# Weights read in place at register addresses, instead of through a staging tile that GpSimd fills

## The chip, the cores and the metric

The kernel runs on one core of one Trainium2 chip. The metric is the time of one execution on the device in microseconds (us); lower is better.

## The reference, cut to what matters

Two layers of a graph network run over 6250 nodes and 100000 edges, each followed by a residual sum and a layer norm. The change lies in the first one:

```python
msg_1 = x @ W_m1.T + b_m1                 # 6250 x 96, one row for each node
msg_2 = x @ W_m2.T + b_m2
msg_e = edge_attr @ W_me.T + b_me
msg = relu(msg_1[row] + msg_2[col] + msg_e)        # row is src, col is dst
msg = relu(msg @ W_net.T + b_net)                  # 100000 x 96
agg = segment_max(msg, row, num_segments=6250)
out = x @ W_o1.T + b_o1 + (agg @ W_o2.T + b_o2)
```

## The kernel before, in words

Each stage of the kernel is a block in which the five engines run programs of their own, tied by semaphores. `pipeline` (L46) writes such a program: each engine has stage functions with a lag, step t calls each of them for item t - lag, the first steps and the last ones are written out, and those between are a hardware loop whose body holds four steps. In the written-out steps the values that waits compare with are constants; in the loop an instruction computes most of them (`wait`, L89, its `wait_ge` on L92).

An earlier stage (its loop runs from about 190 to 1170 us) has put the edges in the order of their source node, cut into 832 chunks of 128 edges, each of them within one block of 128 nodes. For each edge it has stored `msg_2[col] + msg_e` in DRAM (`edge_in_src_order`), and each edge's node within its block in `src_row`.

The stage that changes is the src-ordered one (L1363 on, 1205 to 1700 us). It has G = 832 / 4 = 208 steps of four chunks each:

- SyncE loads 512 rows of `edge_in_src_order` (`u_in`, L1397) and the broadcast node numbers (`rowt`, L1395).
- VectorE makes the one-hot `oh` (node against edge, L1423) and `same` (L1425).
- GpSimd reads the four block starts of the step from `sf_row` into registers (`offsets`, L76, its load on L78) and copies the block's slice of `m1` into the staging tile `m1_s` (L1411), one copy for each chunk. `m1` is `msg_1` of all nodes, kept in SBUF as three bf16 limbs of F = 96 columns side by side; the copy moves them as 144 f32 words.
- TensorE (`pre`, L1451) transposes `u_in` into a PSUM bank (`turn_u`, L1447) and adds to it, for each of four chunks, three products of a limb as weights and the one-hot as the moving operand (L1458): 12 products of 128 columns. ScalarE applies the relu (L1483). TensorE multiplies by `W_net` (`net`, L1465), VectorE scans the running maximum (L1434), TensorE transposes it (`turn`, L1471), ScalarE copies it out and stores it (L1489, L1493).

TensorE calls in step t: `net` for t - 3, `turn` for t - 5, `pre` for t - 1. Before L1458 it waits for `oh_ready` (L1454) and `m1_ready` (L1455). Buffers are four deep in SBUF and two deep in PSUM.

TensorE already uses register addresses for moving operands elsewhere: in the edge stage (`product`, L1254: L1262 and L1266) and in the last large stage (`pre`, L1784: L1791 and L1796).

Of the kernel before, what the change touches and what calls it, by code (L numbers as in the profile page):

```python
# [15 lines left out]
P = 128  # L16
# [3 lines left out]
F32 = mybir.dt.float32  # L20
BF16 = mybir.dt.bfloat16
# [54 lines left out]
def offsets(nc, engine, row, last):  # L76

    _, values = nc.values_load_multi_w_load_instructions(row, engines=[engine], min_val=0, max_val=last,  # L78
                                                         skip_runtime_bounds_check_because="the table holds block starts only")
    return values  # L80
# [8 lines left out]
def wait(eng, sem, value):  # L89

    if not (isinstance(value, int) and value <= 0):
        eng.wait_ge(sem, value)  # L92

def pass_waits(eng, passed):

    eng.sem_inc(passed, 1)
# [24 lines left out]
def gnn(nc, E, x, xT, src, dst, edge_attr, wm12, bm12, w_e, w_net, b_net, wo1, wo2, bo,  # L122
# [34 lines left out]
    def sb(scope, name, shape, dt=F32):  # L157
        return scope.enter_context(nc.sbuf_tensor(name, shape, dt))
# [4 lines left out]
    def sem(scope, name):  # L163
        return scope.enter_context(nc.semaphore(name))
# [4 lines left out]
    with whole:  # L169
# [53 lines left out]
        with layer0:  # L223
# [1139 lines left out]
            with ExitStack() as t:  # L1363
# [1 line left out]
                rowt = sb(t, "rowt", [P, 4, LEAD + 4 * P], BF16)  # L1365
                same = sb(t, "same", [F, 4, 4 * P], BF16)
                oh = sb(t, "oh_b", [P, 4, 4 * P], BF16)
                m1_s = sb(t, "m1_s", [P, 4, 4, 3 * F // 2])
                msg = sb(t, "msg", [F + 1, 4, 4 * P])
                top = sb(t, "top", [F, 4, 4 * P])  # L1370
                row = sb(t, "row", [P, 4, 4, F])
# [2 lines left out]
                ps_top = [ps(t, f"ps_top{k}", [P, 4, P]) for k in range(2)]  # L1374
                u_in = [sem(t, f"u_in{k}") for k in range(4)]
                row_in = [sem(t, f"row_in{k}") for k in range(4)]
                m1_ready = sem(t, "m1_ready")
                passed_pool = sem(t, "passed_pool")
                one_set = sem(t, "one_set")
                oh_ready = sem(t, "oh_ready_b")  # L1380
                same_ready = sem(t, "same_ready")
# [8 lines left out]
                with nc.Block() as block:  # L1390
                    @block.sync
                    def _(sp):
                        def load(i, u, n):
                            wait(sp, same_ready, i - 3)
                            sp.dma_start(rowt[:, u, :], bcast(loc_d[0:1, bass.ds(4 * P * i, LEAD + 4 * P)], P, LEAD + 4 * P)).then_inc(row_in[u], 16)  # L1395
                            wait(sp, u_turned, i - 3)
                            sp.dma_start(u_in_s[:, u], u_d[bass.ds(4 * P * i, 4 * P), :].rearrange("(j p) f -> p j f", p=P)).then_inc(u_in[u], 16)  # L1397

                        pipeline(sp, G, [(0, load)])

                    @block.gpsimd
                    def _(pool):
                        nc.gpsimd.memset(msg[F:F + 1].rearrange("f u e -> f (u e)"), 1.0).then_inc(one_set, 1)

                        def stage(i, u, n):

                            wait(pool, pre_ready, i - 3)
                            pass_waits(pool, passed_pool)
                            at = offsets(nc, mybir.EngineType.Pool, sf_row[0:1, bass.ds(4 * i, 4)], (NB - 1) * 3 * F // 2)
                            for j in range(4):  # L1410
                                last = nc.gpsimd.tensor_copy(m1_s[:, u, j, :], m1[:].bitcast(F32)[:, bass.ds(at[j], 3 * F // 2)])  # L1411
                            last.then_inc(m1_ready, 1)
                        pool.wait_ge(one_set, 1)
                        pipeline(pool, G, [(0, stage)])

                    @block.vector
                    def _(dve):
                        v = nc.vector

                        def onehot(i, u, n):  # L1420
                            dve.wait_ge(row_in[u], 16 * (n + 1))
                            wait(dve, pre_ready, i - 3)
                            v.tensor_scalar(oh[:, u, :], rowt[:, u, LEAD:], node_c[:], None, ALU.is_equal).then_inc(oh_ready, 1)  # L1423
                            wait(dve, top_ready, i - 3)
                            v.tensor_tensor(same[:, u, :], rowt[0:F, u, LEAD:], rowt[0:F, u, LEAD - 1:LEAD - 1 + 4 * P],  # L1425
                                            ALU.is_equal).then_inc(same_ready, 1)

                        def scan(i, u, n):
                            dve.wait_ge(net_ready, i + 1)
                            dve.wait_ge(same_ready, i + 1)  # L1430
                            wait(dve, top_turned, i - 3)
                            wait(dve, top_ready, i)
                            first = isinstance(i, int) and i == 0
                            v.tensor_tensor_scan(top[:, u, :], same[:, u, :], ps_net[u % 2][:],  # L1434
                                                 0.0 if first else top[:, (u - 1) % 4, 4 * P - 1:4 * P],
                                                 ALU.mult, ALU.max).then_inc(top_ready, 1)
                        pipeline(dve, G, [(4, scan), (0, onehot)])

                    @block.tensor
                    def _(pe):  # L1440
                        m = nc.tensor

                        def turn_u(i, u, n, to):
                            pe.wait_ge(u_in[u], 16 * (n + 1))
                            wait(pe, msg_ready, i - 1)
                            for j in range(4):
                                mm = m.matmul(to[:, P * j:P * j + P], u_in_s[:, u, j, :], ident[:],  # L1447
                                              start=(j == 0), stop=False, is_transpose=True, skip_group_check=True)
                            mm.then_inc(u_turned, 1)

                        def pre(i, u, n):  # L1451
                            to = ps_pre[u % 2]
                            turn_u(i, u, n, to)
                            pe.wait_ge(oh_ready, i + 1)  # L1454
                            pe.wait_ge(m1_ready, i + 1)  # L1455
                            for j in range(4):
                                for k in range(3):
                                    mm = m.matmul(to[:, P * j:P * j + P], m1_s[:, u, j, :].bitcast(BF16)[:, F * k:F * k + F], oh[:, u, P * j:P * j + P],  # L1458
                                                  start=False, stop=(k == 2), skip_group_check=True)
                            mm.then_inc(pre_ready, 1)  # L1460

                        def net(i, u, n):
                            wait(pe, top_ready, i - 1)
                            pe.wait_ge(msg_ready, i + 1)
                            m.matmul(ps_net[u % 2][:], wnet_s[:], msg[:, u, :], start=True, stop=True).then_inc(net_ready, 1)  # L1465

                        def turn(i, u, n):
                            pe.wait_ge(top_ready, i + 1)
                            wait(pe, row_ready, i - 1)
                            for j in range(4):  # L1470
                                mm = m.transpose(ps_top[u % 2][:, j, 0:F], top[:, u, P * j:P * j + P], ident[0:F, 0:F])  # L1471
                            mm.then_inc(top_turned, 1)
                        pe.wait_ge(one_set, 1)
                        pipeline(pe, G, [(3, net), (5, turn), (1, pre)])

                    @block.scalar
                    def _(act):
                        s = nc.scalar

                        def first(i, u, n):  # L1480
                            act.wait_ge(pre_ready, i + 1)
                            wait(act, net_ready, i - 3)
                            s.activation(msg[0:F, u, :], ps_pre[u % 2][:], ACT.Relu).then_inc(msg_ready, 1)  # L1483

                        def rows(i, u, n):
                            act.wait_ge(top_turned, i + 1)
                            s4, n4 = past(row_out, u, n, 4)
                            wait(act, s4, 16 * n4)
                            s.copy(row[:, u], ps_top[u % 2][:, :, 0:F]).then_inc(row_ready, 1)  # L1489

                        def store(i, u, n):
                            act.wait_ge(row_ready, i + 1)
                            act.dma_start(s_d[bass.ds(4 * P * i, 4 * P), :].rearrange("(j p) f -> p j f", p=P), row[:, u]).then_inc(row_out[u], 16)  # L1493
                        pipeline(act, G, [(6, store), (5, rows), (1, first)])
                        for k in range(4):
                            act.wait_ge(row_out[k], 16 * len(range(k, G, 4)))
# [574 lines left out]
```

## Time and profile before

| | us |
|---|---|
| median of 3 runs | 2836.42 |
| lowest, highest | 2833.95, 2842.11 |
| span of the profiled execution | 2838.6 |
| busy in it: TensorE / its weight loads | 2320.7 / 2014.7 |
| VectorE / ScalarE / GpSimd | 2036.0 / 1000.7 / 1860.7 |

The profiled execution is one of its own; only its span is given, and it lies inside the runs. The rows further down come from it.
### The profile page before, as it was taken

The page shows a single profiled execution, that of the slowest core. Times are in us where ns is not written, and L with a number is a line of the kernel's source. Part 1 is how long each engine was busy: PE and PEld are TensorE (multiplying, and loading weights), DVE is VectorE, ACT ScalarE, POOL GpSimd, SP SyncE. Part 2 cuts the span into 40 slices and gives each one's busy share as a digit, 9 for nine tenths or more (in the row PEclk, how much of TensorE's full clock was granted, in tenths as well). Part 3 has the DMA queues.
Part 4 walks back from the last instruction along what each step waited for, and adds up shares of the span by engine and source line. Part 5 has one row for each costly group of instructions (what it writes and reads, how often), then busy time and mean ns, then how long its engine had stood idle before and what let it go on. Part 6 is the DMA issues. An engine that isn't in the chain of part 4 may idle for free. (4 is left out here: it accounts for less than half of the span.)

```text
span 2838.6 us, 89638 instructions
## 1 busy us (share of the span) xinstructions
PE 2320.7 (82%) x22430; PEld 2014.7 (71%) x22431; DVE 2036.0 (72%) x9631; ACT 1000.7 (35%) x2286; POOL 1860.7 (66%) x2595
## 2 busy tenths in 40 slices
PE   7778888888888888799999988876677777777777
PEld 6578777777777777477777766766677666777777
DVE  8678777777777777777787877566666666666666
ACT  7334333333333333144444447222222222222225
POOL 1047777777777777654444437677777777777774
PEclk9789999999999999899999998899999999999999
DMA  5021111111111111188888973222222222222221
GB/s 187 29 57 47 45 45 45 45 45 45 45 45 45 45 45 48 35 218 228 226 226 225 227 194 78 54 54 54 54 54 54 53 54 54 54 55 54 55 53 46
DMA packets 582003, 236.10 MB, mean 83 GB/s; under 512 B 512256, under 2 KB 553772, under 8 KB 581676
## 3 DMA queue, kind: packets, MB, share of 16 engines
q1 hardware_dynamic: 298020, 98.53, 15.3%
q0 software_dynamic: 52736, 93.92, 11.6%
q10 hardware_dynamic: 231176, 42.79, 7.5%
q8 instruction: 34, 0.56, 0.1%
q14 instruction: 37, 0.30, 0.0%
HBM read 142.39 MB, written 98.65 MB: 85 GB/s over the span
## 5 line engine op out<-in xcount | busy, mean ns | idle before, releaser
L1041 POOL DMA_INDIRECT edge_in_src_order<-u,place x784 | 756.6, 965 | 259.9 <-issue 185.2
L1714 POOL DMA_INDIRECT a_rows<-src_table,idx x782 | 742.2, 949 | 248.8 <-issue 237.9
L1791 PE MATMUL ps_h<-a_rows,ident 128*128 x1664 | 237.8, 286 | 247.3 <-SPq L1723 185.4
L1791 PEld LDWEIGHTS ps_h<-a_rows,ident 128*128 128x128 f32 x1664 | 202.6, 192 | 278.9 <-issue 278.7
L1411 POOL COPY m_s<-m 128x144 f32 x832 | 234.0, 325 | 244.0 <-PE ps_pre L1458 242.9
L1831 ACT ACTIVATE h<-ps_h 128x512 f32<-128x512 f32 x208 | 124.2, 597 | 743.6 <-PE ps_h L1796 653.9
L1760 DVE TENSOR_SCALAR ohd_f<-iota_b,dloc_c 128x128 f32<-128x128 bf16 x832 | 199.1, 312 | 209.8 <-PE ps_s L1805 204.1
L1434 DVE TENSOR_TENSOR_SCAN top<-same,top,ps_net 96x512 f32<-96x512 bf16 x207 | 264.1, 1276 | 97.9 <-PE ps_net L1465 97.6
L1335 ACT COPY u<-ps_u 128x384 f32<-128x384 f32 x196 | 93.7, 478 | 604.1 <-DMA edge_in_src_order<-u,place 581.7
L1258 PE MATMUL ps_u<-we_s,attrT 128*128 128x384 f32 x392 | 173.8, 525 | 158.9 <-ACT u L1335 158.9
L1748 DVE TENSOR_TENSOR hsumT<-hsumT,ps_s 128x128 f32 x832 | 238.2, 286 | 84.4 <-DVE deg L1750 1.8
L1796 PE MATMUL ps_h<-bpart,dstT_b 128*128 x1664 | 240.5, 289 | 1.6 <-ACT dstT_b L1825 1.6
L1262 PEld LDWEIGHTS ps_u<-m,dstT 128*128 128x128 f32 x1568 | 193.2, 192 | 66.8 <-issue 63.0
L1805 PE MATMUL ps_s<-ohd_f,h 128*128 128x128 f32 x1664 | 224.5, 279 | 0.5 <-DVE deg L1750 0.3
L1465 PE MATMUL ps_net<-msg,wnet_s 97*96 97x512 f32 x416 | 218.5, 607 | 0.0
L1266 PE MATMUL ps_u<-more,ident 128*128 x1568 | 218.1, 282 | 0.0
L1123 DVE CUSTOM_DVE_ANT_0 junk<-ps_cnt,ohlo_a 128x64 bf16<-128x64 f32 x784 | 129.1, 221 | 121.5 <-PE ps_cnt L1232 121.3
L1796 PEld LDWEIGHTS ps_h<-bpart,dstT_b 128*128 128x128 f32 x1664 | 206.8, 195 | 6.1 <-issue 1.8
L1805 PEld LDWEIGHTS ps_s<-ohd_f,h 128*128 128x128 f32 x1664 | 207.3, 196 | 1.0 <-ACT h L1831 0.5
L1262 PE MATMUL ps_u<-m,dstT 128*128 x1568 | 203.2, 273 | 0.0
L1266 PEld LDWEIGHTS ps_u<-more,ident 128*128 128x128 f32 x1568 | 190.6, 192 | 0.0
L1258 PEld LDWEIGHTS ps_u<-we_s,attrT 128*128 128x128 f32 x392 | 58.8, 189 | 185.2 <-issue 185.2
(357 smaller groups left out, 5400.8 us busy)
## 6 DMA issues: line engine op xcount, KB each, us to landing
u_in<-edge_in_src_order SPq DMA_DIRECT2D x208, 192.0 KB, 3.4
running_max<-row ACTq DMA_DIRECT2D x208, 192.0 KB, 4.2
rowt<-src_row SPq DMA_DIRECT2D x208, 130.0 KB, 3.7
key_b<-edge_keys ACTq DMA_DIRECT2D x832, 1.5 KB
edge_in_src_order<-u,place POOLq DMA_INDIRECT x784, 2.2
a_rows<-src_table,idx POOLq DMA_INDIRECT x782
edge_attributes<-in_edge_attr SPq DMA_DIRECT2D x8, 784.0 KB, 12.0
attr_in<-edge_attributes SPq DMA_DIRECT2D x196, 32.0 KB, 1.9
```

Source lines behind the costliest of these rows:

```text
L1041: pool.indirect_dma_start(u_d, bass.IndirectOffsetOnAxis(place[:, u, j:j + 1], 0), ur[:, u, j, :], None).then_inc(sent[u], 16)
L1258: m.matmul(ps_u.rearrange("p j f -> p (j f)"), attrT[:, u, :], we_s[:].rearrange("p j f -> p (j f)"), start=True, stop=False, skip_group_c ...
L1262: m.matmul(ps_u[:, j, :], dstT[:, u, j, :], m2[:, bass.ds(at[j], F)], start=False, stop=False, skip_group_check=True)
L1266: mm = m.matmul(ps_u[:, j, :], ident[:], more[:, bass.ds(of[j], F)], start=False, stop=True, skip_group_check=True)
L1411: last = nc.gpsimd.tensor_copy(m1_s[:, u, j, :], m1[:].bitcast(F32)[:, bass.ds(at[j], 3 * F // 2)])
L1434: v.tensor_tensor_scan(top[:, u, :], same[:, u, :], ps_net[u % 2][:], 0.0 if first else top[:, (u - 1) % 4, 4 * P - 1:4 * P], ALU.mult, AL ...
L1465: m.matmul(ps_net[u % 2][:], wnet_s[:], msg[:, u, :], start=True, stop=True).then_inc(net_ready, 1)
L1714: pool.indirect_dma_start(a_rows[:, 4 * u + j, :], None, a_d, bass.IndirectOffsetOnAxis(idx[:, u % 4, j:j + 1], 0)).then_inc(got[u % 4], 16)
L1748: adds.add(v.tensor_tensor(at, at, ps_s[k][:, j, :], ALU.add))
L1791: m.matmul(ps_h[k][:, j, :], ident[:], a_rows[:].rearrange("p c d -> p (c d)")[:, bass.ds(slot[j], D)], start=(j == 0), stop=False, skip_g ...
L1796: mm = m.matmul(ps_h[k][:, j, :], dstT[:, k, j, :], bpart[:, bass.ds(at[j], D)], start=False, stop=True, skip_group_check=True)
L1805: mm = m.matmul(ps_s[k][:, j, :], h[:, u, j, :], ohd[:, u, j, :], start=True, stop=True)
```

## The change

The tile `m1_s`, GpSimd's copies and the two semaphores go; GpSimd keeps its memset of a row of ones. TensorE loads the four block starts of a step into its own registers, between the transposes of `u_in` and the wait for the one-hot, and takes each limb straight from `m1`, at an address computed from the register.

```diff
@@ -1365,7 +1365,6 @@
-                m1_s = sb(t, "m1_s", [P, 4, 4, 3 * F // 2])
@@ -1374,8 +1373,6 @@
-                m1_ready = sem(t, "m1_ready")
-                passed_pool = sem(t, "passed_pool")
@@ -1402,16 +1399,6 @@
                         nc.gpsimd.memset(msg[F:F + 1].rearrange("f u e -> f (u e)"), 1.0).then_inc(one_set, 1)
 
-                        def stage(i, u, n):
-
-                            wait(pool, pre_ready, i - 3)
-                            pass_waits(pool, passed_pool)
-                            at = offsets(nc, mybir.EngineType.Pool, sf_row[0:1, bass.ds(4 * i, 4)], (NB - 1) * 3 * F // 2)
-                            for j in range(4):
-                                last = nc.gpsimd.tensor_copy(m1_s[:, u, j, :], m1[:].bitcast(F32)[:, bass.ds(at[j], 3 * F // 2)])
-                            last.then_inc(m1_ready, 1)
-                        pool.wait_ge(one_set, 1)
-                        pipeline(pool, G, [(0, stage)])
@@ -1451,11 +1438,12 @@
                         def pre(i, u, n):
                             to = ps_pre[u % 2]
                             turn_u(i, u, n, to)
+                            at = offsets(nc, mybir.EngineType.PE, sf_row[0:1, bass.ds(4 * i, 4)], (NB - 1) * 3 * F // 2)
                             pe.wait_ge(oh_ready, i + 1)
-                            pe.wait_ge(m1_ready, i + 1)
-                            for j in range(4):
+                            for j in range(4):
+                                part = m1[:].bitcast(F32)[:, bass.ds(at[j], 3 * F // 2)].bitcast(BF16)
                                 for k in range(3):
-                                    mm = m.matmul(to[:, P * j:P * j + P], m1_s[:, u, j, :].bitcast(BF16)[:, F * k:F * k + F], oh[:, u, P * j:P * j + P],
+                                    mm = m.matmul(to[:, P * j:P * j + P], part[:, F * k:F * k + F], oh[:, u, P * j:P * j + P],
                                                   start=False, stop=(k == 2), skip_group_check=True)
                             mm.then_inc(pre_ready, 1)
```

## Rows read from the trace of the kernel before

**Rows 1.** Busy time of each engine by stretch, with granted clock, DMA share and GB/s
```profile
1225.00:1690.00 465.00, 465.00 (x4399) 354.37 (x4398) 370.67 (x599) 213.75 (x400) 222.12 (x792) 1.00 0.88 225
...
2302.00:2342.00 40.00, 27.79 (x224) 26.10 (x224) 23.87 (x113) 8.59 (x16) 30.25 (x33) 1.00 0.28 54
```

**Rows 2.** Groups by line and form, 1225 to 1690 us: busy, mean ns | idle before
```profile
L1434 DVE TENSOR_TENSOR_SCAN top<-same,top,ps_net 96x512 f32<-96x512 bf16 x200 | 255.2, 1276 | 94.3 <-PE ps_net L1465 94.3
L1411 POOL COPY m_s<-m 128x144 f32 x792 | 222.1, 324 | 238.9 <-PE ps_pre L1458 238.9
...
L1458 PE MATMUL ps_pre<-oh_b,m_s 128*96 128x128 bf16 x2399 | 166.6, 219 | 0.0
```

**Rows 3.** Timeline, two neighbouring steps of the stage: start us, us, engine, line
```profile
1403.04 0.83 PE L1458 MATMUL ps_pre<-oh_b,m_s 128*96 128x128 bf16 x12
...
1405.37 0.83 PE L1458 MATMUL ps_pre<-oh_b,m_s 128*96 128x128 bf16 x12
```

**Rows 4.** TensorE's sequencer by line, one loop turn (1400.1:1409.4): ns min/median/max, first, last start
```profile
L70 PEldq ALU_OP  x1: 32/32/32, 1400.1 to 1400.1; - x1
L70 PEldq COMPARE_BRANCH  x1: 207/207/207, 1400.2 to 1400.2; - x1
L70 PEldq FUSED_REGOPS  x1: 50/50/50, 1400.5 to 1400.5; - x1
...
L92 PEldq EVENT_SEMAPHORE  x5: 51/51/51, 1401.0 to 1407.7; - x5
L92 PEldq ALU_OP  x3: 32/32/32, 1400.8 to 1402.7; - x3
L92 PEldq FUSED_REGOPS  x1: 37/37/37, 1403.2 to 1403.2; - x1
...
L1464 PEldq ALU_OP  x2: 32/34/36, 1400.6 to 1402.6; - x2
L1464 PEldq EVENT_SEMAPHORE  x2: 51/51/51, 1404.8 to 1407.1; - x2
...
L1468 PEldq FUSED_REGOPS  x1: 51/51/51, 1400.7 to 1400.7; - x1
...
L1444 PEldq ALU_OP  x1: 36/36/36, 1400.9 to 1400.9; - x1
L1444 PEldq FUSED_REGOPS  x1: 37/37/37, 1403.1 to 1403.1; - x1
...
L1454 PEldq ALU_OP  x4: 32/32/36, 1401.2 to 1407.9; - x4
...
L1455 PEldq EVENT_SEMAPHORE  x4: 51/51/51, 1401.3 to 1408.0; - x4
```

**Rows 5.** The same view in the edge stage, 809.7 to 811.2 us
```profile
L1262 PEldq FUSED_REGOPS  x4: 37/37/37, 809.8 to 810.1; - x4
...
L78 PEldq ALU_OP  x1: 32/32/32, 810.3 to 810.3; - x1
L78 PEldq TENSOR_LOAD <-xs_row x1: 347/347/347, 810.4 to 810.4; - x1
...
L1266 PEldq FUSED_REGOPS  x4: 37/37/37, 810.8 to 811.1; - x4
```

**Rows 6.** Products of the last large stage by line, whole span
```profile
L1791 PE MATMUL ps_h<-a_rows,ident x1664: 275/275/423, 1798.7 to 2768.9; 128*128 x185
...
L1805 PE MATMUL ps_s<-ohd_f,h x1664: 274/275/421, 1805.1 to 2772.1; 128*128 128x128 f32 x185
```

**Rows 7.** TensorE's sequencer on L1444, whole span (one for each loop turn)
```profile
L1444 PEldq ALU_OP  x48: 36/36/36, 1242.4 to 1680.4; - x48
```

**Rows 8.** VectorE's one-hots and TensorE's waits on L1455, 1205 to 1402.8 us
```profile
L1423 DVE TENSOR_SCALAR oh_b<-rowt,node_c x85: 323/324/465, 1208.3 to 1401.5; 128x512 bf16<-128x512 bf16 x85
...
L1455 PEldq EVENT_SEMAPHORE  x84: 51/51/51, 1209.1 to 1401.3; - x84
```

**Rows 9.** Timeline, TensorE's first work of the stage
```profile
1209.08 1.06 PE L1447 MATMUL ps_pre<-ident,u_in 128*96 128x128 f32 x4 [5.88 <-DMA u_in<-edge_in_src_order]
```

## The prediction

> **What bounds the kernel now.** I read the stage first in the busy times by stretch [rows 1]. From 1225 to 1690 us TensorE (PE) is busy for all of the 465.00 us at a granted clock of 1.00, VectorE for 370.67, GpSimd (POOL) for 222.12, ScalarE for 213.75. Then I read who waits for whom, in the groups by line [rows 2]. GpSimd's copies stood idle for 238.9 us until an L1458 product came free, so GpSimd waits for TensorE and not the other way. VectorE's scan waited 94.3 us for TensorE's L1465. The twelve L1458 products of a step, 219 ns each, had no idle time in front of them at all. A busy PE in this profile is modelled, so I checked it by the spacing: one step's L1458 group starts at 1403.04 and the next one's at 1405.37 [rows 3]. That is 2.33 us a step, and 4 x 2.33 = 9.31 us for one turn of the hardware loop, which holds four steps. The array sets the pace; GpSimd is on no path.
>
> Last I read the work of TensorE's own sequencer, which is counted as busy nowhere. In one turn of the loop it runs 27 instructions of its own [rows 4]: 3 on L70, 4 on L1464, 1 on L1468, 9 on L92, 2 on L1444, 4 on L1454 and 4 on L1455. It runs ahead of the array: it passed L1455 at 1401.3 [rows 4], for products that the array began at 1403.04 [rows 3]. That lead of 1.7 us is why these 27 cost nothing today.
>
> **Removed.** GpSimd's copies (792 of the 832 lie in the stretch, 222.1 us busy [rows 2]), their register loads and their waits. They lie beside TensorE's work, so the gain is 0. At the stage's start nothing is gained either: TensorE's first transpose waited for the u_in transfer and not for GpSimd [rows 9]. TensorE's wait on m1_ready (L1455) goes: 4 of the 27. VectorE may gain if GpSimd no longer reads beside it, but it has 465.00 - 370.67 = 94.33 us to spare in the stretch [rows 1], and what would be late next is still TensorE.
>
> By the Trainium skill, "SBUF — State Buffer", section "Who interferes with whom", a VectorE instruction with two SBUF inputs and a GpSimd one that reads SBUF hold each other up, which speaks for the change (L1425 is such an instruction); the same section says that TensorE never waits on anyone. By that rule too the sum gains nothing, since VectorE isn't the bound.
>
> **Added, on TensorE's sequencer.** For each step: one load of four values into registers, one operation for its index, and one address operation for each of twelve weight loads. I take twelve and not four, since the three limbs of a slice lie F columns apart and each weight load takes a whole address; in the kernel before, each matrix product with a moving address (L1262, L1266, L1791) has its own address operation, for instance 4 on L1262 for 4 products [rows 5]. For a loop turn that is 4 + 4 + 48 = 56 more, 4 fewer for L1455: 27 + 56 - 4 = 79.
>
> The cost of one is not its duration of 32 to 51 ns but the step to the next. A chain of the edge stage shows it [rows 5]: four address operations from 809.8, an ALU_OP at 810.3, a load at 810.4, four more address operations from 810.8 to 811.1. The load's step is 0.4 us; the other eight steps take 1.3 - 0.4 = 0.9 us, 0.113 each, most of them with four TensorE instructions sent in between. In the stage itself, from L70's FUSED_REGOPS at 1400.5 to L1455 at 1401.3, seven steps take 0.8 us, 0.114 each [rows 4], and between them lie none, four or eight TensorE instructions; so sending these is nearly free, and I price them inside the step. The loop's branch takes from 1400.2 to 1400.5, 0.3 us.
>
> Today's sequencer chain is thus 26 x 0.113 + 0.3 = 3.2 us of 9.31. With the change it is 74 x 0.113 + 4 x 0.4 + 0.3 = 8.36 + 1.6 + 0.3 = 10.26 us. That is more than the array needs. The array's queue can't hide it: it hides a late start, not a lasting rate. The excess is 10.26 - 9.31 = 0.95 us a turn, and the loop makes 48 turns (L1444's ALU_OP [rows 7]): 45.6 us. The 16 steps in front of the loop have constants for their waits: 17 short steps and a load, 17 x 0.113 + 0.4 = 2.3 us against 2.33, so nothing. Once, the lead of 1.7 us is used up: 45.6 - 1.7 = 44 us.
>
> By the Trainium skill, "Perfetto Trace Analysis", section "Sequencer-only Instruction (DRAIN, etc)", the profiler reports the execution alone, while fetch, decode and the wait stay out. The trace agrees: 37 ns reported, 0.113 us from one to the next. Summed by the reported durations, the 48 address operations would be 48 x 37 = 1.8 us a turn, the whole chain would stay under 9.31, and the change would look free.
>
> **The new weight address itself.** No row shows a weight load at a register address. The nearest are products whose moving operand has one (L1791) and whose operands have none (L1805): both 275 ns [rows 6]. I take 0, as this is the same kind of operand of the same engine. The upper bound is one more sequencer step for each such load, 48 x 0.113 = 5.4 us a turn, 260 us in all. Below nothing I see no way, for the same columns are loaded.
>
> **The wait that moves.** The wait for the one-hot (oh_ready) today stands at a weight load, in the array's queue. Behind the change an address operation comes first, so the sequencer itself will stand there, and queued behind it are the twelve products, the next step's L1465 and the transposes; ScalarE's L1483 and VectorE's scan wait for those. VectorE had begun its 85th one-hot at 1401.5 while the sequencer passed its 84th L1455 at 1401.3 [rows 8]: the 84th one-hot is a step of 2.33 us older. With its 0.32 us it ended near 1399.5, a cover of about 1.8 us, and it grows as the sequencer gets later. Cost 0; without that cover VectorE's pace would enter, which at 370.67 / 465 of the time is still the quicker one [rows 1].
>
> **The clock.** With gaps of under 0.3 us a step the granted clock should stay: in the last stage TensorE is busy for 27.79 of 40 us and has 1.00 [rows 1].
>
> DMA engines are busy for 0.88 of the stretch [rows 1], and TensorE waits for none of them there; a slower pace only eases that.
>
> **Rivals.** (a) Hidden after all. If a short step cost 0.100 us (L70's ALU_OP at 1400.1 to its branch at 1400.2 [rows 4]), the chain would be 7.4 + 1.6 + 0.3 = 9.3 us, just what the array takes, and the time would be 2836. Less than 0.101 a step decides for it. The same result comes if one address operation served the three limbs of a slice: 32 fewer, 3.6 us less. Against it: 0.113 and 0.114 in two places; one operation for each address everywhere else. For it: the margin is 10%. (b) The address operations are longer. On L70 and L1468 an operation shows 50 to 51 ns in place of 37 [rows 4]; the bitcasts and the limb's offset may need that: 48 x 0.013 = 0.6 us a turn, 30 us more, 2910. (c) The register-addressed weight load costs a step of its own, by the bound above: up to 3140. In a sentence for itself: the Trainium skill, "TensorE: Matmul & The Clock Gate", section "Part 2: What happens when you issue a matmul", gives about 62 ns per matmul where the sequencer's firmware must translate it rather than the hardware decoder; an estimate by that figure, for 12 x 208 weight loads, would be 155 us more; no row here shows such a cost. (d) Faster: GpSimd's reads of m1 slow the array's own pace. Twelve L1458 products stretch over 0.83 us [rows 3], the last one 0.219 of it [rows 2], so they start 0.61 / 11 = 0.0555 us apart, while 128 columns at 2.4 GHz are 0.0533. If all of a step is slowed by these 4% and GpSimd is why, 0.04 x 2.33 x 208 = 19 us come back, 2817, from the point on where the sequencer keeps up. I see no row that says GpSimd is why.
>
> **How the numbers follow.** The profiled execution's span is 2838.6 us, inside the runs shown (2833.95 to 2842.11), so I add to their median, 2836.42: 2836.4 + 44 = 2880. Chances: the forecast with its own range of 2855 to 2914, (b) in it, 0.72; (a) 0.18; (c) 0.05; (d) 0.05. About 0.3%, 8.5 us, is what a measurement can tell from no change: faster 0.05, same 0.17, slower 0.78. The own range's low end is a short step of 0.107 us (9.75 us a turn, 21 us over), its high end the packed operations of (b). The whole range goes from 2836, to take in (a), to 2914.
>
> **What would show it.** L1458 with 2496 address operations in TensorE's queue and L78 with 208 loads of sf_row; the stage about 44 us longer; idle time ended by "issue" in front of L1458's weight loads; about 2.54 us from one step to the next; GpSimd's busy time down by about 233 us (832 / 792 x 222.1); VectorE's idle time in front of the scan up by about 0.2 us a step; the other stages unchanged. I'd be wrong if the spacing stays at 2.33 (a), if L1458's weight loads stand further than 0.12 us apart (c), or if the address operations number 832.

## The result, and the profile after

| | before | changed |
|---|---|---|
| median, us (4 runs each) | 2835.18 | 2915.58 |
| lowest, highest | 2832.48, 2842.11 | 2912.72, 2918.50 |
| ratio, 95% interval | | 1.0275 [1.0258, 1.0292] |
| span of the profiled execution | 2838.6 | 2916.8 |

The change costs 80 us. The sign and the mechanism were as forecast; the forecast of 2880 us named 44 us where 80 were measured, and the result lies 1.6 us above the upper end of the range.

The time came from one place. This is TensorE's sequencer in the changed kernel over the whole span, on the line that computes a wait's value once in each loop turn (L1431, which answers to L1444 in [rows 7]), then GpSimd's first fetch of the next stage, in the changed kernel and in the kernel before:

```profile
L1431 PEldq ALU_OP  x48: 36/36/36, 1242.8 to 1756.3; - x48
```

```profile
L1545 POOL DMA_INDIRECT agg_all<-running_max,last_i x49: 940/944/1001, 1777.6 to 1837.6; - x49
```

```profile
L1557 POOL DMA_INDIRECT agg_all<-running_max,last_i x49: 951/955/1029, 1700.9 to 1761.4; - x49
```

Between the first and the last of 48 turns lie 47: (1756.3 - 1242.8) / 47 = 10.93 us a turn, where [rows 7] give (1680.4 - 1242.4) / 47 = 9.32. That is 1.61 x 48 = 77 us. The first fetch of the next stage stood at 1700.9 before and stands at 1777.6 now, also 77 us later. The spans differ by 78, so hardly anything is left for the other stages.

One turn of the loop in the changed kernel, the sequencer by line, from 1406.15 to 1417.02 us (the count, ns min/median/max, first and last start), answers to [rows 4]:

```profile
L70 PEldq COMPARE_BRANCH  x1: 208/208/208, 1406.2 to 1406.2; - x1
...
L92 PEldq EVENT_SEMAPHORE  x5: 51/51/51, 1407.1 to 1414.8; - x5
...
L1442 PEldq ALU_OP  x4: 32/32/36, 1407.7 to 1415.5; - x4
L1446 PEldq FUSED_REGOPS  x48: 46/46/51, 1407.8 to 1416.9; - x48
L78 PEldq FUSED_REGOPS  x4: 46/48/60, 1407.2 to 1414.9; - x4
L78 PEldq TENSOR_LOAD <-sf_row x4: 331/333/337, 1407.3 to 1415.0; - x4
```

There are 48 address operations, four loads and four operations for their index, as counted ahead; with those not shown the turn holds 79 instructions of the sequencer. The address operations show 46 ns and not the 37 of [rows 5]. One step's twelve, seen alone (1407.7 to 1409.3):

```profile
L1446 PEldq FUSED_REGOPS  x12: 46/46/46, 1407.8 to 1409.2; - x12
```

Eleven steps in 1.4 us are 0.127 us each, against 0.113 in the sum.

The trace also shows the array coming to wait for these operations. First a step ahead of the loop (window 1235.9 to 1238.1), where the steps still take 2.33 us, then the step just shown (the weight loads of the window 1406.7 to 1409.4):

```profile
L1446 PEldq FUSED_REGOPS  x12: 46/46/46, 1236.0 to 1237.4; - x12
L1446 PEld LDWEIGHTS ps_pre<-oh_b,m x12: 123/123/123, 1237.3 to 1237.9; 128*96 x12
```

```profile
L1446 PEld LDWEIGHTS ps_pre<-oh_b,m x12: 119/123/123, 1408.3 to 1409.3; 128*96 x12
```

Ahead of the loop the last weight load starts 0.5 us behind its address operation: the sequencer is ahead. In the loop it starts 0.1 us behind it here, and in no step more than 0.2: the sequencer's lead is gone, and the array takes each product as it comes.

Busy times by stretch and the groups by line, from inside the stage (they answer to [rows 1, 2]):

```profile
1250.00:1750.00 500.00, 484.00 (x4032) 369.03 (x4030) 339.66 (x550) 195.94 (x367) 0.00 (x0) 1.00 0.77 193
```

```profile
L1421 DVE TENSOR_TENSOR_SCAN top<-same,top,ps_net 96x512 f32<-96x512 bf16 x190 | 242.4, 1276 | 162.8 <-PE ps_net L1453 162.8
...
L1446 PE MATMUL ps_pre<-oh_b,m 128*96 128x128 bf16 x2280 | 192.7, 227 | 0.0
...
L1412 DVE TENSOR_TENSOR same<-rowt 96x512 bf16<-96x512 bf16 x190 | 79.0, 416 | 0.0
```

This is what makes such a loss hard to see. TensorE is "busy" for 484 of 500 us at a granted clock of 1.00, L1446 has no idle time in front of it, and its 219 ns became a mean of 227: the products are thinly spread and their modelled durations cover the gaps. Only the spacing shows it. The timeline has the L1446 group of a step behind the loop's branch stretched from 0.83 us [rows 3] to 1.17 (the three groups ahead of it to 1.04, 0.94 and 0.91), with twelve products as before:

```profile
1408.42 1.17 PE L1446 MATMUL ps_pre<-oh_b,m 128*96 128x128 bf16 x12
```

The idle time that there is stands in front of the next product, L1453 (the same view, 1225 to 1740 us):

```profile
L1453 PE MATMUL ps_net<-msg,wnet_s 97*96 97x512 f32 x380 | 204.3, 619 | 15.7 <-DVE top L1421 8.0 <-issue 7.7
```

The 8.0 us put down to VectorE's scan are an inference that misleads, at least in the one case looked at: in the timeline that scan ran from 1405.03 for 1.28 us, to 1406.31, while L1453 began at 1406.72, behind the loop's branch.

GpSimd's 0.00 in the stretch is the whole of what was removed, and VectorE waits longer for TensorE: 162.8 us for 190 scans, 0.86 each, against 94.3 for 200 [rows 2], 0.47 each.

### The profile page after: what moved, and what is told of

It reads as the page before. It is cut to its first block and busy times, and to the rows that moved or that the text cites. A ratio compares the mean times of both kernels' runs of the same rounds, so it can differ in the third digit from the quotient of the medians.

```text
span 2916.8 us, 89794 instructions
## 1 busy us (share of the span) xinstructions
PE 2370.3 (81%) x22430; PEld 2047.8 (70%) x22431; DVE 2035.0 (70%) x9631; ACT 1000.0 (34%) x2286; POOL 1622.2 (56%) x1762
## 5 line engine op out<-in xcount | busy, mean ns | idle before, releaser
L1421 DVE TENSOR_TENSOR_SCAN top<-same,top,ps_net 96x512 f32<-96x512 bf16 x207 | 264.1, 1276 | 175.0 <-PE ps_net L1453 174.7
L1545 POOL DMA_INDIRECT agg_all<-running_max,last_i x49 | 46.3, 945 | 586.3 <-POOLq L1387 571.7
L1262 PEld LDWEIGHTS ps_u<-m,dstT 128*128 128x128 f32 x1568 | 194.0, 192 | 66.7 <-issue 63.4
L1453 PE MATMUL ps_net<-msg,wnet_s 97*96 97x512 f32 x416 | 223.5, 619 | 16.5 <-DVE top L1421 8.3
L1446 PE MATMUL ps_pre<-oh_b,m 128*96 128x128 bf16 x2496 | 210.8, 227 | 0.0
L1262 PE MATMUL ps_u<-m,dstT 128*128 x1568 | 204.0, 273 | 0.0
L1446 PEld LDWEIGHTS ps_pre<-oh_b,m 128*96 x2496 | 200.7, 123 | 3.3
```

The source lines that it names most:

```text
L1262: m.matmul(ps_u[:, j, :], dstT[:, u, j, :], m2[:, bass.ds(at[j], F)], start=False, stop=False, skip_group_check=True)
L1446: mm = m.matmul(to[:, P * j:P * j + P], part[:, F * k:F * k + F], oh[:, u, P * j:P * j + P], start=False, stop=(k == 2), skip_group_check= ...
```

## The experiments

Two theories. **S:** TensorE's sequencer has more to do in a loop turn than the array, and its instructions set the pace. **W:** a weight load at a register address costs the array itself, 80 us / 2496 = 32 ns each. A third, **P,** asks whether the removed copies had slowed something, so that a gain hides in the loss.

Eight of the ten kernels ran on a chip where the kernel before took 3781 us (beside the three `slices` kernels and `no_copies`) and 3826 us (beside `one_address`, `idle_ops`, `copies_kept` and `bf16_row`). Other stages took longer there: in `slices2` the granted clock from 190 to 700 us was 0.84, and L1262 of the edge stage ended at 1582 us, where the kernel before had a clock of 1.00 and 1167 us; why is not shown. The stage in question did not: each kernel of these eight whose sequencer keeps up has the same loop turn of 9.32 us. So differences in us and loop turns are compared, and a ratio is given beside them. `limbs8` and the changed kernel's second run stand beside 2839 us.

**Some slices at registers, the others staged** (against the kernel before; here two of four, `slices2`):

```diff
-                            for j in range(4):
+                            for j in range(2, 4):
                                 last = nc.gpsimd.tensor_copy(m1_s[:, u, j, :], ...
...
+                            at = offsets(nc, mybir.EngineType.PE, sf_row[0:1, bass.ds(4 * i, 4)], (NB - 1) * 3 * F // 2)
...
                             for j in range(4):
+                                part = (m1[:].bitcast(F32)[:, bass.ds(at[j], 3 * F // 2)] if j < 2 else m1_s[:, u, j, :]).bitcast(BF16)
...
```

> One slice of four (3 of 12 weight loads) at a register address, the other three copied by GpSimd as before. Theory S (TensorE's sequencer has too many instructions): a loop turn of the changed kernel takes it 10.93 us; with 36 address operations fewer at 0.1255 us and four waits more at 0.126 us it would take 6.9 us, under the array's 9.32, so the time of the kernel before, 2835 us within 5. Theory W (a weight load at a register address costs the array time itself, 80 us / 2496 = 32 ns each): a quarter of 80 us, 2855 us.

> Two slices of four at register addresses (6 of 12 weight loads), two copied by GpSimd. Theory S: 10.93 - 24 x 0.1255 + 4 x 0.126 = 8.4 us a loop turn for the sequencer, still under 9.32, 2835 us within 5. Theory W: half of 80 us, 2875 us.

> Three slices of four at register addresses (9 of 12 weight loads), one copied by GpSimd. Theory S: 10.93 - 12 x 0.1255 + 4 x 0.126 = 9.93 us a loop turn, 0.61 over the array's 9.32, times 48: 29 us, 2864 us; the step from two to three slices is where it turns. Theory W: three quarters of 80 us, 2895 us.

Measured: one slice 3782.15 against 3780.68 us, ratio 1.0003 [0.9991, 1.0016]; two slices 3778.50, 0.9993 [0.9981, 1.0005]; three slices 3807.77, 27 us more, 1.0066 [1.0044, 1.0087]. The once-a-turn instruction of two slices, then of three:

```profile
L1444 PEldq ALU_OP  x48: 36/36/36, 1658.8 to 2096.7; - x48
```

```profile
L1444 PEldq ALU_OP  x48: 36/36/36, 1657.4 to 2120.2; - x48
```

437.9 / 47 = 9.32 us and 462.8 / 47 = 9.85 us. Half of the weight loads at register addresses cost nothing; a further quarter costs 0.53 x 48 = 25 us. W's 20, 40 and 60 us are out, for it would have each load cost the same. S expected 9.93 and overstated it by 0.08: with 0.1255 for an operation, 9.85 leaves 0.107 us for each of the four waits on `m1_ready` that stand here and not in the changed kernel, where 0.126 was taken.

**At the knee** (`limbs8`, two slices and two limbs of the third):

```diff
...
                                 for k in range(3):
+                                    here = m1[:].bitcast(F32)[:, bass.ds(at[j], 3 * F // 2)]
+                                    part = (here if 3 * j + k < 8 else m1_s[:, u, j, :]).bitcast(BF16)
...
```

> Eight of the twelve weight loads of a step at register addresses, the last four from GpSimd's staging tile: 32 address operations in a loop turn. With 36 (three slices) the sequencer's turn measured 9.85 us. Theory S, linear: 9.85 - 4 x 0.1255 = 9.35 us, at the knee, against 9.32 for the array: the loop turn of the profile between 9.32 and 9.36 us, 0 to 2 us more in all, no difference that can be measured. Theory W: 8 / 12 of 80 us, 53 us more.

Measured: 2840.08 against 2838.64 us, 1.0003 [0.9993, 1.0013].

```profile
L1444 PEldq ALU_OP  x48: 36/36/36, 1240.9 to 1680.5; - x48
```

439.6 / 47 = 9.35 us. Four address operations fewer than with three slices took (462.8 - 439.6) / 47 / 4 = 0.123 us each off the turn. So the turn is flat at 9.32 us up to 24 operations, begins to rise at 32 and grows by the price of each one from there: a sequencer that runs ahead until its own work is longer than the array's. The last stretch, from 36 to 48, fits the same price only with the waits at 0.107 us.

**All weight loads at registers, a third of the address operations** (`one_address`, against the changed kernel). Of one slice's three products with the same address only the first has an address operation:

```diff
-                                    mm = m.matmul(to[:, P * j:P * j + P], part[:, F * k:F * k + F], ...
+                                    mm = m.matmul(to[:, P * j:P * j + P], part[:, 0:F], ...
```

> The changed kernel, all 12 weight loads of a step at register addresses, but the three products of a slice all read its first limb, so that one address operation serves three of them (the other two limbs are left out of the sum): 16 address operations in a loop turn in place of 48. Theory S: 10.93 - 32 x 0.1255 = 6.9 us a turn, under 9.32, so 2835 us within 5. Theory W: 2915 us, since the weight loads at register addresses are as many as in the changed kernel.

Measured: 3828.22 against 3826.38 us, 1.0004 [0.9994, 1.0013]. L1446 over the whole span, and the once-a-turn instruction (437.9 / 47 = 9.32 us):

```profile
L1446 PEld LDWEIGHTS ps_pre<-oh_b,m x2496: 122/123/203, 1644.9 to 2128.2; 128*96 x192
...
L1446 PEldq FUSED_REGOPS  x832: 46/46/51, 1644.6 to 2126.5; - x167
...
L1431 PEldq ALU_OP  x48: 36/36/36, 1678.3 to 2116.2; - x48
```

2496 weight loads at register addresses with 832 operations cost nothing; with 2496 operations they cost 80 us. This is the run that decides between S and W. The price of the weight address itself, which no row of before showed, is 0 within the interval, and the weight loads last 123 ns either way.

**The sequencer's work without any register address** (`idle_ops`, against the kernel before):

```diff
                             pe.wait_ge(m1_ready, i + 1)
+                            for q in range(4):
+                                pass_waits(pe, passed_pre[q])
                             for j in range(4):
                                 for k in range(3):
+                                    pass_waits(pe, passed_pre[j])
                                     mm = m.matmul(to[:, P * j:P * j + P], m1_s[:, u, j, :]...
```

> The kernel before, staging and copies and static addresses kept, with 16 increments of unused semaphores more for each step in TensorE's instruction stream (four ahead of the products, one ahead of each): work for the sequencer alone. Theory S: 64 more in a loop turn at 0.126 us are 8.1 us, on top of about 3.4: 11.5 us against the array's 9.32, times 48: about 100 us more, 2935 us. Theory W (the register-addressed weight load is what costs): 2835 us.

Measured: 3990.31 against 3826.38 us, 164 us more, 1.0424 [1.0407, 1.0442]. The once-a-turn instruction, and one step's 16 increments (1751.3 to 1753.7):

```profile
L1445 PEldq ALU_OP  x48: 36/36/36, 1691.4 to 2282.2; - x48
...
L97 PEldq EVENT_SEMAPHORE  x16: 51/51/51, 1751.3 to 1753.6; - x16
```

590.8 / 47 = 12.57 us a turn, and (12.57 - 9.32) x 48 = 156 us of the 164; the steps outside the loop have the increments too and were not taken apart. The cause is confirmed without one register address. The size is not what I expected, 164 us in place of about 100: fifteen steps take 2.3 us, 0.153 each in place of 0.126. 64 x 0.153 = 9.8 leaves 2.8 us for the other 23. What the sequencer does in a step beyond the reported 46 or 51 ns is shown by none of these runs; they show that the step's length goes with the kind of operation.

**The copies alone, taken away and put back.** `no_copies`, against the kernel before:

```diff
...
-                        pipeline(pool, G, [(0, stage)])
+                        nc.gpsimd.memset(m1_s[:].rearrange("p u j f -> p (u j f)"), 0.0).then_inc(m1_ready, 1)
...
-                            pe.wait_ge(m1_ready, i + 1)
+                            pe.wait_ge(m1_ready, 1)
```

> The kernel before without GpSimd's copies: the staging tile is set to zero once, so msg_1 is left out of the messages; TensorE's instructions stay. Theory S: GpSimd was on no path, 2835 us within 5. Rival P (GpSimd's reads of m1 slow the array or VectorE, so that the removal alone is a gain which the changed kernel hides under a larger loss): 2817 us or less.

Measured: 3782.36 against 3780.68 us, 1.0001 [0.9991, 1.0010]. From inside the stage:

```profile
1660.00:2080.00 420.00, 420.00 (x3976) 320.19 (x3975) 335.09 (x542) 193.52 (x361) 0.00 (x0) 1.00 0.88 226
```

```profile
L1416 DVE TENSOR_TENSOR same<-rowt 96x512 bf16<-96x512 bf16 x180 | 75.0, 417 | 0.0
```

```profile
L1435 PEldq ALU_OP  x48: 36/36/36, 1650.8 to 2088.8; - x48
```

The loop turn is 438.0 / 47 = 9.32 us, with the copies or without.

`copies_kept`, the changed kernel with the copies running into a tile of their own (with one more wait on GpSimd, for its own copies of three steps ago):

> The changed kernel with GpSimd's copies left running into a tile that nobody reads. Theory S: 2915 us within 5, GpSimd is on no path. Rival P (the copies slow TensorE or VectorE): above 2925 us.

Measured: 3901.52 against 3826.38 us, 75 us more, 1.0199 [1.0182, 1.0216]; 512.9 / 47 = 10.91 us a turn:

```profile
L1445 PEldq ALU_OP  x48: 36/36/36, 1678.0 to 2190.9; - x48
```

In `no_copies` TensorE is busy throughout and in `copies_kept` it starves, and the copies change neither. P is out, and with it my rival (d).

**The length of an address operation** (`bf16_row`, against the changed kernel): the block starts are doubled once into a row of their own, and m1 is sliced in bf16.

```diff
-                                part = m1[:].bitcast(F32)[:, bass.ds(at[j], 3 * F // 2)].bitcast(BF16)
...
-                                    mm = m.matmul(to[:, P * j:P * j + P], part[:, F * k:F * k + F], ...
+                                    mm = m.matmul(to[:, P * j:P * j + P], m1[:, F * k:][:, bass.ds(at[j], F)], ...
...
```

> The changed kernel with a table of block starts that is doubled once ahead of the stage, so that m1 is sliced in bf16 without the two bitcasts and an address operation has one term less. Theory S with the address operation's length as what I mis-sized: its 46 ns go to 37 as in the other stages, its step from 0.124 to 0.115 us, 48 x 0.009 = 0.43 us a turn, 21 us less, 2894 us. If the operation's length doesn't matter to the step, or theory W: 2915 us.

Measured: 3903.10 against 3826.38 us, 77 us more, 1.0198 [1.0178, 1.0217]: no better than `copies_kept` on the same chip. One step's operations, 1751.95 to 1753.45 us, and the turn:

```profile
L1448 PEldq FUSED_REGOPS  x12: 37/46/51, 1752.0 to 1753.4; - x12
...
L1434 PEldq ALU_OP  x48: 36/36/36, 1683.1 to 2192.7; - x48
```

The edit hardly did what it was meant to: the median is still 46 ns, and the turn is 509.6 / 47 = 10.84 us, 0.07 to 0.09 less than the changed kernel's 10.91 and 10.93 in its two profiles. Set beside `one_address`, it shows why. There the operations have the bitcasts and no limb's offset, and 46 ns; here two of three have an offset and no bitcasts, and 46 ns; only the first limb of a slice has neither, for instance the one at 1750.4:

```profile
L1448 PEldq FUSED_REGOPS  x1: 42/42/42, 1750.4 to 1750.4; - x1
```

So either of the two brings an operation to 46 ns, and taking away the bitcasts shortens a third of them by 4 ns. The 37 ns that I had expected are the shortest of the twelve and not the rule; what makes one 37 and another 42 stays open.

**The changed kernel once more,** on a chip where the kernel before took 2838.64 us:

> The changed kernel on the chip of the experiments, so that the kernels with its address operations can be set against it directly. Theory S: its loop turn 10.93 us as before, 77 to 80 us more than the kernel before on this chip; nothing in it depends on the other stages.

Measured: 2916.89 us, 78 us more, 1.0275 [1.0258, 1.0292]. L1431's 48 lie from 1244.2 to 1757.2, 10.91 us a turn.

## Why the prediction was right, and where its size was off

- **What bounds the kernel before,** the array at 9.32 us a loop turn with GpSimd on no path: right. The removal alone gains nothing (`no_copies`), nor does putting the copies back cost anything.
- **The count,** 79 sequencer instructions with 48 address operations: right, to the instruction. Rival (a), one operation for a slice's three limbs, isn't what the change does; `one_address` shows that it would have hidden the whole cost.
- **The price of a short step:** the term that was mis-sized. I took 0.113 us from a chain whose operations report 37 ns, and it holds for those. The changed kernel's report 46 and step by 0.127 in the row above; over the 48 that is 48 x 0.014 = 0.67 us a turn, the whole of 10.93 - 10.26. So the rest of the turn came out as summed: 10.93 - 48 x 0.127 = 4.83 us, against 10.26 - 48 x 0.113 = 4.84. Times 48 the 0.67 us are 32 us of the 36 that the forecast was short. I had seen it coming as rival (b), priced it at 0.6 us a turn, 30 us, and kept it for the upper end. It should have been in the centre: the kernel's other addresses are a start and a base, this one has a limb's offset and a change of type on top, and the rows of L70 and L1468 showed what more terms cost.
- **The lead of 1.7 us** that I took off once isn't seen: 77 us of the loop and 77 us at the next stage's first fetch leave no room for it. It was the lead of the kernel before. The changed kernel's sequencer, with 2.3 us of work for a step of 2.33, came to the loop with little to use up: 0.5 us at the last weight load of the step shown above.
- **The steps in front of the loop:** nothing expected, and the whole of the stage's 77 us is the loop's.
- **The signs named ahead:** the counts came out. The step is 10.93 / 4 = 2.73 us and not 2.54, and VectorE's scan waits 0.39 us a step more and not 0.2, both by the price above. One sign was wrong: the idle time put down to "issue" does not stand in front of the twelve weight loads, whose line has 3.1 us of idle time from 1225 to 1740 us; the products thin out instead. The twelve loads of the step shown start 1.0 / 11 = 0.09 us apart, under the 0.12 that was named for rival (c).
- **The weight address itself:** taken as 0, between 0 and 260 us; 0 it is (`one_address`, `slices2`). Rival (c) is out. The cost that the Trainium skill gives for a matmul that the sequencer's firmware must translate ("TensorE: Matmul & The Clock Gate", section "Part 2: What happens when you issue a matmul") is not seen with a weight address in a register either. Of the prediction's estimate of 155 us nothing shows: `one_address`, with as many such weight loads, measured 2 us, and the changed kernel's turn adds up without it.
- **The wait that moves:** the twelve operations of a step, which now stand behind the wait for the one-hot, follow each other at one pace, and no idle time in the stage is put down to VectorE's one-hot. Cost 0 stands. It wasn't tried by an experiment of its own.
- **The clock:** granted 1.00 before and after in the stage.
- **Rival (d),** GpSimd slowing the array: out, by `no_copies`. The Trainium skill's rule on VectorE instructions with two SBUF inputs beside GpSimd's reads ("SBUF — State Buffer", section "Who interferes with whom") is another matter, and a mean can't test it: `same` has 417 ns before and in `no_copies` and 416 in the changed kernel because in the steady steps it doesn't meet the copies. Timeline of the kernel before, 1400 to 1403 us:

```profile
1401.74 0.42 DVE L1425 TENSOR_TENSOR same<-rowt 96x512 bf16<-96x512 bf16 x1
...
1402.23 1.12 POOL L1411 COPY m_s<-m 128x144 f32 x4 [1.20 <-PE ps_pre L1458]
```

The copies wait for the products and so fall beside the scan, which takes 1276 ns with and without them. At the stage's start the two do meet (1210 to 1211 us):

```profile
1209.72 1.56 POOL L1411 COPY m_s<-m 128x144 f32 x5
...
1210.60 0.51 DVE L1425 TENSOR_TENSOR same<-rowt 96x512 bf16<-96x512 bf16 x1
```

There `same` takes 0.51 us in place of 0.42. Four of the 208 take 0.51 to 0.52 us, all of them at the stage's start and with copies beside them for their whole length. The lengths over the whole span (ns min/median/max), before and in `no_copies`:

```profile
L1425 DVE TENSOR_TENSOR same<-rowt x208: 412/417/521, 1208.6 to 1688.0; 96x512 bf16<-96x512 bf16 x104
```

```profile
L1416 DVE TENSOR_TENSOR same<-rowt x208: 414/416/420, 1617.1 to 2096.4; 96x512 bf16<-96x512 bf16 x104
```

Without copies none is longer than 420 ns. The trace agrees with the rule, at about 0.1 us each time that they meet. That happens too seldom to matter here: `no_copies`, without any of it, is no faster.

- **The knee:** I put it at 0.101 us a step. With the measured price of 0.12 to 0.13 us it lies at 32 address operations (`limbs8`, 9.35 us). Two slices at register addresses are free, and they halve GpSimd's copies, which nobody waits for; so no mix can be expected to beat the kernel before, since the array, and nothing that this change touches, holds the 9.32 us.

## What to carry to other kernels

An address in a register is free for the array and not for the engine's sequencer: count its instructions in a loop turn, price each at the step from one start to the next rather than at its reported length, and compare that sum with the array's time for the same turn. Take the step from operations with as many terms as the new ones will have, and put that step, not the shortest one seen, in the centre of the forecast. Moving work off an idle engine gains nothing by itself, and a TensorE that still reads 97% busy may be waiting for its own sequencer: look at the spacing of the groups, and at how far each weight load stands behind its address operation. Before a mean is read as "these two don't disturb each other", look in the timeline whether they ever run at the same time.

## What the hardware showed that I had not expected

- Increments of a semaphore by the sequencer (`idle_ops`) step by 0.153 us at a reported 51 ns, more than an address operation at 46 ns with 0.127.
- The cost is flat and then rises from a sharp knee: 24 and 32 address operations a turn leave it at 9.32 and 9.35 us, 36 make it 9.85, 48 (with four waits fewer) make it 10.93. In these runs a sequencer ahead of the array hides everything up to the array's own time and nothing beyond.
- Where VectorE's `same` runs beside GpSimd's copies it takes 0.51 us in place of 0.42, and the longest in `no_copies` is 420 ns.
